# Second transformer layer: lane 1 of each turn four stages behind lane 0

## The chip, the core and the metric

The kernel runs on one core of one Trainium2 chip. The metric is the time of one execution on the device in microseconds; the median of the runs is taken. The engines of the core run their own instruction lists in order and meet only through semaphores: TensorE (PE), VectorE (DVE), ScalarE (ACT), GpSimd (POOL) and SyncE (SP), which issues most DMAs.

## What is computed

Two layers over an input x of 8 batches, 512 tokens and 256 features, in float32. The change touches the second layer alone, up to its end:

```python
# per batch: hidden 256, H = 16 heads of DH = 16, M = 64 random features
dg, db, ug, ub = cond @ (down_gamma, down_beta, up_gamma, up_beta)
h  = x + relu(x @ (down * dg + db)) @ (up * ug + ub)
q, k = feature_map(h @ Wq.T + bq), feature_map(h @ Wk.T + bk)   # exp(proj - norm) + 1e-6
v  = h @ Wv.T + bv
kv, ksum = k^T v, sum(k)             # per head
x  = x + (q @ kv / (q @ ksum)) @ Wo.T + bo
y  = x @ weight(cond) + bias(cond)
s  = max|y| / 127 per token;  y8 = round(y / s)
x  = x + (y8 @ Wq8) * s * weight_scale + bias
```

The first layer ends in a mixture of experts. Its last step, to add each token's two expert rows with their weights, is done by the second layer: it gathers the rows by index.

## The kernel before

After the first layer, `layer1` loads its weights and works through the 8 batches in four turns of two. A turn is `body(b2, more)`: three turns are a hardware loop with `more` true, the fourth stands behind it with `more` false. The two batches of a turn are lanes 0 and 1. Each lane has its own buffers and its own four PSUM banks; the lanes share no data, only the engines. A barrier of all engines ends each turn.

Each engine's part of a turn is a generator `lane(n, v, s)` that yields a stage number before it emits the instructions of that stage. `in_stages` (line 1560) makes one generator per lane and walks the stages: for each stage it lets lane 0 and then lane 1 emit what is due. So every engine's list is stage by stage, lane 0 ahead of lane 1 within a stage.

The stages, with their numbers: 0 transposes of x (line 1720), 1 down projection (1725), 2 up projection (1730), 3 and 4 the projections for K and Q (1742; ScalarE's biases and squares of Q in pieces of 32 partitions, line 1847), 5 V and the norms of K (1749, 1752), 6 to 9 the feature maps, two of eight parts a stage (TensorE 1766 and 1771, VectorE 1910, ScalarE's exponentials 1853 and 1855, the 1e-6 added by POOL at 1688 or VectorE at 1916 and 1919), 10 KV sums (1783), 11 their transposes (1790), 12 denominators and outputs (1797, 1802; VectorE's reciprocal 1941), 13 broadcast of the reciprocals (1808) and the product (1946), 14 output projection (1715), 15 transposes (1708), 16 the conditioned projection (1715) and VectorE's quantising block (1958 to 1970), 17 transposes of the quantised rows (1708), 18 the last projection (1715) and VectorE's scaling and sum (1974, 1978). `STAGES` is 19.

In a turn with `more`, the rows for the same lane's next batch are fetched: SP waits for the KV sums of lane 0, loads its indices and residual, then the same for lane 1 (lines 1666 to 1669). In stage 12 VectorE casts the indices (1581) and POOL issues eight indirect DMAs a lane (1588); in stage 16 VectorE adds the weighted rows ahead of the quantising block (1608); in stage 18 POOL waits for the transfers and resets them. SP stores lane 0's result, then lane 1's (1670 to 1674).

Of the kernel before, what the change touches and what calls it, by code (L numbers as in the profile page):

```python
# [55 lines left out]
def spread(ap, at, n, step=0):  # L56

    dims = [list(d) for d in ap.ap]
    dims.insert(at, [step, n])
    return bass.AP(ap.tensor, ap.offset, dims)  # L60
# [1445 lines left out]
ST_IN, ST_DN, ST_UP, ST_QK = range(4)  # L1506
ST_V, ST_KF = ST_QK + 2, ST_QK + 3
POOL_KF = (0, 2, 3, 5, 7)
QK_OUT = (2, 3, 0, 1, 2, 3)
ST_KV, ST_KVT, ST_O, ST_OT, ST_X3, ST_X3T, ST_Y, ST_Q, ST_ACC, STAGES = range(ST_KF + 4, ST_KF + 14)  # L1510

def layer1(nc, a, out, bank, ident, sb_in, Sems, chain_of, x1_d, gate_d, y_d, prow_d, wdec_d, PR, R1, n1):
# [3 lines left out]
    with l1:  # L1517
# [19 lines left out]
        LANES = 2  # L1537
# [22 lines left out]
        def in_stages(s, program):  # L1560

            live = [program(n, lane_bufs[n], lambda name, n=n: s(f"{name}_{n}")) for n in range(LANES)]
            due = [next(g) for g in live]
            for stage in range(STAGES):
                for n, g in enumerate(live):
                    while due[n] is not None and due[n] <= stage:
                        due[n] = next(g, None)  # L1570
            assert due == [None] * LANES

# [76 lines left out]
        def body(b2, more):  # L1649

            sctx = ExitStack()
            with sctx:
                s = Sems(sctx, "c")

                with nc.Block() as block:
# [20 lines left out]
                    @block.gpsimd  # L1676
                    def _(pool):
                        def lane(n, v, s):
                            yield ST_UP
                            pool.memset(v["kv"][:], 0.0).then_inc(s("kv0"), 1)  # L1680
                            pool.memset(v["kd"][:], 0.0).then_inc(s("kv0"), 1)
                            pool.tensor_tensor(v["xb"][:], v["x2"], spread(row("bo"), 1, T), ALU.add).then_inc(s("xb_ok"), 1)

                            for i in POOL_KF:
                                yield ST_KF + i // 2
                                pool.wait_ge(s("kf_in"), i + 1)
                                part = v["kf"][:, i // 2, 8 * (i % 2):8 * (i % 2) + 8, :]
                                pool.tensor_scalar(part, part, 1e-6, None, ALU.add).then_inc(s("kf_ok"), 1)  # L1688
                            yield ST_O
                            if more:  # L1690
                                gather_rows(pool, v, s)
                            yield ST_X3
                            pool.wait_ge(s("x3_ok"), 1)
                            pool.tensor_tensor(v["xb"][:], v["x3"], spread(row("bias"), 1, T), ALU.add).then_inc(s("x3b_ok"), 1)
                            yield ST_ACC
                            if more:
                                gathered(pool, s)
                        in_stages(s, lane)

                    @block.tensor  # L1700
                    def _(pe):
                        def lane(n, v, s):
# [31 lines left out]
                            for i in range(2 + 2 * K2):  # L1734
# [5 lines left out]
                                for m in range(K2):  # L1740
                                    w = wkv[:, 0, m, i * P:(i + 1) * P] if i < 2 else wqs[:, m, (i - 2) * P:(i - 1) * P]
                                    mm = pe.matmul(bk[QK_OUT[i]][:], w, v["hcT"][:, m, :], start=(m == 0), stop=(m == K2 - 1))  # L1742
                                mm.then_inc(s("qk_mm"), 1)
# [29 lines left out]
                            yield ST_KV  # L1773
                            pe.wait_ge(s("kf_ok"), len(POOL_KF))
                            pe.wait_ge(s("kf_ok2"), 8 - len(POOL_KF))
                            for g in range(2):
# [47 lines left out]
                            pe.wait_ge(s("qbT_ok"), 2)  # L1824
                            tokens_major(v["qbT"], wqb, "acc_mm")
                        in_stages(s, lane)

                    @block.scalar
                    def _(act):
                        def lane(n, v, s):  # L1830
# [9 lines left out]
                            for i in range(2 + 2 * K2):  # L1840
                                if i == 4:
                                    yield ST_QK + 1
                                if i >= 2:
                                    src = bk[QK_OUT[i]]
                                    act.wait_ge(s("qk_mm"), i + 1)
# [19 lines left out]
                            for m in range(K2):  # L1865
                                act.wait_ge(s("qbT_mm"), m + 1)
                                act.copy(v["qbT"][:, m, :], bk[m][:].bitcast(BF16)[:, 0:S]).then_inc(s("qbT_ok"), 1)
                        in_stages(s, lane)

                    @block.vector  # L1870
                    def _(dve):
                        def lane(n, v, s):
# [17 lines left out]
                            for i in range(2):  # L1890
                                dve.wait_ge(s("qk_mm"), i + 1)
                                dve.tensor_scalar(v["kT"][:, i, :], bk[QK_OUT[i]][:], kcol[:, i:i + 1], None, ALU.add).then_inc(s("ksq_ok"), 1)
                                dve.wait_ge(s("ksq_ok"), 2 * i + 1)
# [13 lines left out]
                            for i in range(8):  # L1907
# [4 lines left out]
                                                  spread(v["kn"][:, i // 2, i % 2, :], 2, M), ALU.add).then_inc(s("kf_sub"), 1)  # L1912
                                if i and i - 1 not in POOL_KF:
                                    dve.wait_ge(s("kf_in"), i)
# [190 lines left out]
```

## Time and profile before

| what | value |
|---|---|
| median of 3 runs | 3029.67 us (3029.49 to 3034.95) |
| the profiled execution | 3033.5 us, its span 3031.6 us |
| TensorE busy | 2256.5 us, 74% |
| VectorE busy | 1509.8 us, 50% |
| ScalarE busy | 1025.9 us, 34% |
| POOL busy | 890.6 us, 29% |
| mean granted clock of TensorE | 0.793 of full speed |
| turns of the second layer start at | 2456.3, 2604.0, 2750.8 and 2898.3 us |

Times in the rows are microseconds from the start of the span. A row of a timeline gives the start, the duration of the merged instructions, the engine, the line, what it writes and reads, how many instructions, and in brackets the idle time of that engine just before it with what ended it.
### The profile page before, as it was taken

Reading aid. Unit: us, or ns where it says so; the run is one execution under the profiler, and the core shown is the slowest. Engines: PE = TensorE matmul, PEld = TensorE weight load, DVE = VectorE, ACT = ScalarE, POOL = GpSimd, SP = SyncE. Lnnn points to the kernel's source line nnn. Section 1 sums busy time; section 2 is a strip of 40 time slices with the busy share of each in tenths; the row PEclk is TensorE's granted clock in tenths of the full one; section 3 lists DMA queues with packets and bytes.
Section 4 is the critical chain, followed back from the end, with each engine's and each line's share of the span. In section 5 each row is a group of like instructions: output and inputs, shape, how many; then the busy total and the mean of one; then the engine's idle time right before and its main releaser. Section 6 shows DMA issues by size and latency. Waiting matters only on the chain. (4 is left out here: it accounts for less than half of the span.)

```text
span 3031.6 us, 33534 instructions
## 1 busy us (share of the span) xinstructions
PE 2256.5 (74%) x11770; PEld 1421.0 (47%) x11770; DVE 1509.8 (50%) x3624; ACT 1025.9 (34%) x2535; POOL 890.6 (29%) x649
## 2 busy tenths in 40 slices
PE   6248877777777778768787777854999959686877
PEld 5125544444444444435444444432777725353544
DVE  2477576565655745746747556431111025453635
ACT  2015443333344334424334334431222233323332
POOL 0345252243334325324325223031000024040412
PEclk9577777778678678677677777876999979798989
DMA  6100010020010010010011002021322131010110
GB/s 216 37 16 1 21 58 1 15 72 7 15 59 20 15 58 22 8 65 22 1 56 37 1 15 70 1 65 37 112 94 94 59 97 43 29 42 29 42 30 15
DMA packets 62448, 128.67 MB, mean 42 GB/s; under 512 B 14420, under 2 KB 39114, under 8 KB 59858
## 3 DMA queue, kind: packets, MB, share of 16 engines
q1 hardware_dynamic: 46426, 76.32, 7.2%
q0 software_dynamic: 15872, 50.35, 5.6%
q8 instruction: 95, 1.56, 0.2%
q14 instruction: 55, 0.45, 0.1%
HBM read 97.17 MB, written 29.46 MB: 42 GB/s over the span
## 5 line engine op out<-in xcount | busy, mean ns | idle before, releaser
L1023 ACT ACTIVATE att_buf<-att_buf,nmin 128x384 f32<-128x384 f32 (+3 forms) x512 | 287.5, 562 | 771.4 <-DVE nmin L1338 764.1
L864 PE MATMUL bank<-kk,qT 32*128 32x512 f32 (+2 forms) x1024 | 356.7, 735 | 88.4 <-DVE nmin L1338 88.4
L695 POOL TENSOR_TENSOR big<-ex_at,kx 128x2048 f32<-128x2048 f32 x64 | 235.1, 3681 | 386.9 <-DVE xt_na L1132 313.1
L891 PE MATMUL bank<-ident,att_buf 128*128 128x128 f32 x1280 | 260.5, 343 | 56.8 <-ACT att_buf L1031 50.6
L1327 DVE TENSOR_TENSOR att_buf<-bank,wdiag 128x128 f32<-128x128 f32 x384 | 93.1, 284 | 322.0 <-PE bank L869 297.5
L644 POOL TENSOR_TENSOR big<-kx 128x1280 f32<-128x1280 f32 x64 | 162.6, 2567 | 300.3 <-ACT kx L963 291.2
L1132 DVE TENSOR_REDUCE xt_na<-big 128x64 f32<-128x1024 f32 x128 | 242.0, 1905 | 2.4 <-POOL big L695 1.6
L905 PE MATMUL bank<-att_buf,vp 128*32 128x128 f32 x2560 | 239.4, 329 | 0.0
L1031 ACT COPY att_buf<-bank 128x384 f32<-128x384 f32 (+3 forms) x512 | 208.6, 409 | 65.7 <-remote 40.7
L891 PEld LDWEIGHTS bank<-ident,att_buf 128*128 128x128 f32 x1280 | 190.2, 181 | 71.0 <-issue 42.5
L864 PEld LDWEIGHTS bank<-kk,qT 32*128 32x128 f32 x1024 | 118.5, 238 | 160.7 <-DVE nmin L1338 120.6
L905 PEld LDWEIGHTS bank<-att_buf,vp 128*32 128x32 f32 x2560 | 144.4, 128 | 65.9 <-issue 51.9
L1471 ACT ACTIVATE hid<-bank,eb 128x320 f32<-128x320 f32 x128 | 67.5, 527 | 241.6 <-PE bank L1446 241.6
L1446 PE MATMUL bank<-eb,ew 128*128 128x320 f32 x512 | 141.0, 437 | 1.7 <-DVE eb L1481 1.7
L1458 PE MATMUL bank<-ew,hid 128*128 128x256 f32 x640 | 139.6, 379 | 0.6 <-ACT hid L1471 0.6
L1338 DVE CUSTOM_DVE_ANT_0 att_buf<-bank,att_buf 128x128 f32<-128x128 f32 (+3 forms) x320 | 137.8, 446 | 0.0
L1688 POOL TENSOR_SCALAR kf<-kf 128x512 f32<-128x512 f32 x40 | 67.4, 1684 | 232.9 <-ACT kf L1853 231.9
L1458 PEld LDWEIGHTS bank<-ew,hid 128*128 128x128 f32 x640 | 121.0, 190 | 17.2 <-ACT hid L1471 1.1
L763 PE MATMUL bank<-cat,wint 128*128 128x512 f32 x256 | 119.2, 616 | 0.7 <-ACT cat L988 0.7
L1446 PEld LDWEIGHTS bank<-eb,ew 128*128 128x128 f32 x512 | 98.3, 192 | 42.4 <-DVE eb L1481 2.1
L856 PE MATMUL bank<-kk,qT 32*128 32x128 f32 x256 | 73.8, 379 | 57.9 <-DVE nmin L1338 31.2
L1111 DVE TENSOR_REDUCE big<-big 128x80 f32<-128x1280 f32 x64 | 86.4, 1349 | 47.2 <-POOL big L644 47.0
(339 smaller groups left out, 4049.2 us busy)
## 6 DMA issues: line engine op xcount, KB each, us to landing
ew<-in_eW SPq DMA_DIRECT2D x16, 1024.0 KB
buf_d<-zero SPq DMA_DIRECT2D x8, 640.0 KB, 7.9
er<-buf_d SPq DMA_DIRECT2D x8, 640.0 KB
y_d<-yy SPq DMA_DIRECT2D x8, 640.0 KB, 9.3
xt_na<-in_xT SPq DMA_DIRECT2D x8, 512.0 KB, 3.9
nA<-in_xN SPq DMA_DIRECT2D x8, 512.0 KB, 4.6
x_d<-x SPq DMA_DIRECT2D x8, 512.0 KB, 3.8
kf<-x_d SPq DMA_DIRECT2D x8, 512.0 KB, 3.2
```

Of the source, the lines that this page charges most:

```text
L644: pool.tensor_tensor(prod[:, lo:hi], spread(kx[:, t, 0:D], 1, hi - lo), spread(kx[:, t, DH * lo:DH * lo + D], 1, hi - lo, DH), ALU.mult)\
L695: pool.tensor_tensor(pv[:, :, c * P:(c + 1) * P].rearrange("p o (h d) -> p o h d", d=DH), spread(ex[:, t, :, 8 * c:8 * c + 8], 3, DH), spr ...
L763: mm = pe.matmul(bank[SIDE[o]][:], wint[:, order[n], o * P:(o + 1) * P], cat[:, n, :], start=(n == 0), stop=(n == 7))
L864: pe.matmul(bank[u % 2][:, 0:n], qT[r:r + 32, g, i * P:(i + 1) * P], kk[r:r + 32, g, T * i * P:T * i * P + n], start=True, stop=False)
L891: mm = pe.transpose(bank[3 + u % 2][:, j * P:(j + 1) * P], pr[:, u % NPR, j * P:(j + 1) * P], ident[:])
L905: mm = pe.matmul(bank[5][r:r + 32, i * P:(i + 1) * P], vp[:, j, p, DH * c:DH * c + 2 * DH], prT[:, (u + x) % 3, j * P:(j + 1) * P], start= ...
L1023: act.activation(pr[:, u % NPR, 0:n], pr[:, u % NPR, 0:n], ACT.Exp, scale=-1.0, bias=nmin[:, u % 4:u % 4 + 1], accum_out=rsum[:, i, h:h + ...
L1031: act.copy(prT[:, u % 3, 0:n], bank[3 + u % 2][:, 0:n]).then_inc(s("prT_ok"), 1)
L1132: dve.tensor_reduce(nA1[:, t, c * w:(c + 1) * w], pv[:, :, c * w:(c + 1) * w].rearrange("p o f -> p f o"), X, ALU.add).then_inc(s("pv_used ...
L1338: dve.tensor_tensor_reduce(dst if x else tiled(dst), lg[:, 0:n] if x else tiled(lg[:, 0:n]), add, 1.0, LARGE, ALU.add, ALU.min, nmin[:, (u ...
L1446: mm = pe.matmul(bank[n % 4][:, 0:W], ew1[:, k % 2, m, o * P:(o + 1) * P], eb[:, k % 2, m, c * W:(c + 1) * W], start=(m == 0), stop=(m == ...
L1458: mm = pe.matmul(bank[4 + n % 4][:, 0:D], hid[:, m, t * P:(t + 1) * P], ew2[:, k % 2, m, :], start=(m == 0), stop=(m == KH - 1))
```

## The change

`in_stages` shifts lane 1 by `LAG` = 4 stages: in its walk, lane n emits stage k when the walk is at k + 4n, and the walk is four stages longer. This holds for the lists of TensorE, ScalarE, VectorE and POOL. SP's list, the instructions themselves, their semaphores and buffers, and the order within each lane are as before.

```diff
 POOL_KF = (0, 2, 3, 5, 7)
+LAG = 4
...
-            for stage in range(STAGES):
+            for stage in range(STAGES + LAG * (LANES - 1)):
                 for n, g in enumerate(live):
-                    while due[n] is not None and due[n] <= stage:
+                    while due[n] is not None and due[n] + LAG * n <= stage:
                         due[n] = next(g, None)
```

## Rows read from the trace of the kernel before

**Rows 1.** The page's first part: TensorE's busy time and share of the span.
```profile
PE 2256.5 (74%) x11770; PEld 1421.0 (47%) x11770; DVE 1509.8 (50%) x3624; ACT 1025.9 (34%) x2535; POOL 890.6 (29%) x649
```

**Rows 2.** Windows, last turn: length, PE, PEld, DVE, ACT, POOL busy, clock, DMA, GB/s.
```profile
2898.30:3031.60 133.30, 111.31 (x656) 65.26 (x656) 62.71 (x114) 49.81 (x82) 27.21 (x18) 0.92 0.06 17
```

**Rows 3.** Timeline of TensorE in the third turn, loads of weights left out.
```profile
2751.07 3.67 PE L1708 MATMUL bank<-ident,kf 128*128 128x128 f32 x16 [9.37 <-PEq L100]
2757.80 5.88 PE L1725 MATMUL bank<-xT,wdn 128*64 128x512 f32 x8 [3.06 <-DVE wup L1883]
...
2767.25 3.70 PE L1742 MATMUL bank<-hcT,wkv 128*128 128x512 f32 x8
...
2774.22 3.60 PE L1742 MATMUL bank<-hcT,wkv 128*128 128x512 f32 x8
...
2790.80 0.67 PE L1749 MATMUL bank<-wkv,hcT 128*128 128x256 f32 x2 [2.68 <-ACT qs L1847]
...
2796.35 0.67 PE L1749 MATMUL bank<-wkv,hcT 128*128 128x256 f32 x2 [0.18 <-ACT qs L1847]
...
2801.58 1.10 PE L1766 MATMUL bank<-orfk,kT 128*128 128x512 f32 x2
...
2829.22 1.08 PE L1783 MATMUL bank<-kf,vn 128*32 128x128 f32 x32
...
2838.12 1.92 PE L1797 MATMUL bank<-qf,kd 128*32 128x512 f32 x16 [0.24 <-DVE kd L1934]
...
2855.20 10.20 PE L1715 MATMUL bank<-wo,xT 128*128 128x256 f32 x32 [4.48 <-DVE xT L1946]
...
2884.78 1.03 PE L1708 MATMUL bank<-identb,yb 128*128 128x128 bf16 x8 [7.32 <-DVE yb L1970]
```

**Rows 4.** Timelines of ScalarE and VectorE in that turn, and one group of VectorE's.
```profile
2779.57 16.63 ACT L1847 ACTIVATE qs<-bank,qscol 32x512 f32<-32x512 f32 x24 [1.34 <-PE bank L1742]
...
2840.12 3.36 DVE L1941 RECIPROCAL k<-bank 128x512 f32<-128x512 f32 x1 [0.84 <-PE bank L1797]
...
2879.86 1.28 DVE L1958 TENSOR_TENSOR qf<-bank,brow 128x512 f32<-128x512 f32 x2
...
2884.03 0.69 DVE L1970 TENSOR_SCALAR yb<-qf 128x1024 bf16<-128x1024 f32 x1
...
2892.08 1.23 DVE L1978 TENSOR_TENSOR qf<-qf,xb 128x1024 f32<-128x1024 f32 x1
...
L1919 DVE TENSOR_SCALAR qf<-qf 128x512 f32<-128x512 f32 x14 | 6.3, 448 | 0.1
```

**Rows 5.** Timelines of TensorE and VectorE in the last turn.
```profile
2898.45 3.67 PE L1708 MATMUL bank<-ident,kf 128*128 128x128 f32 x16 [9.44 <-PEq L100]
...
2985.01 1.92 PE L1797 MATMUL bank<-qf,kd 128*32 128x512 f32 x16 [0.24 <-DVE kd L1934]
...
2995.67 7.07 PE L1715 MATMUL bank<-wo,xT 128*128 128x256 f32 x32
...
3025.71 1.23 DVE L1978 TENSOR_TENSOR qf<-qf,xb 128x1024 f32<-128x1024 f32 x1
```

**Rows 6.** Waits: total us, times, longest; and POOL's first and last gather.
```profile
DVE xT L1946 <- remote: 27.2, 9, 5.2
ACT xT L1859 <- remote: 24.2, 6, 5.7
...
2839.55 1.04 POOL L1588 DMA_INDIRECT kf<-y_d,gidx  x1 [8.04 <-DVE gidx L1581]
...
2858.41 0.94 POOL L1588 DMA_INDIRECT kf<-y_d,gidx  x1 [0.30 <-issue]
```

**Rows 7.** Windows, as in rows 2, over most of the output projection.
```profile
2855.00:2862.00 7.00, 6.80 (x18) 5.42 (x18) 1.52 (x3) 0.00 (x0) 3.44 (x4) 0.55 0.38 96
```

**Rows 8.** Timelines of POOL and TensorE in layer 0, a run of eight transfers.
```profile
1971.01 1.03 POOL L704 DMA_INDIRECT buf_d<-nB,sidx  x1 [86.70 <-DVE sidx L1254]
...
1980.01 0.97 POOL L704 DMA_INDIRECT buf_d<-nB,sidx  x1 [0.30 <-issue]
...
1982.65 0.76 PE L856 MATMUL bank<-kk,qT 32*128 32x128 f32 x2 [4.84 <-remote]
```

## The prediction

> **What bounds the kernel now.** I read the page first, then the second layer alone, since the edit touches nothing else. TensorE is busy 74% of the span [rows 1], but that mixes two layers. The windows by turn narrow it: in the last of the four turns of the second layer TensorE is busy 111.3 of 133.3 us, VectorE 62.7, ScalarE 49.8 [rows 2]. So TensorE bounds the turns, and a lag of one lane can only win back what TensorE waits. The timeline of TensorE in a middle turn (the third) shows where that is [rows 3]. The turn runs from its first transpose at 2751.07 to the end of VectorE's last addition at 2892.08 + 1.23 = 2893.31 [rows 3, 4], which is 142.2 us. The last turn runs from 2898.45 to 3025.71 + 1.23 = 3026.94 [rows 5], 128.5 us, with the same matmuls. Between turns lie some 5 us that the edit leaves alone.
>
> Why is a loop turn 13.7 us longer than the last one? Only loop turns gather the rows for the next turn. From the first denominator matmul to the first matmul of the output projection a loop turn takes 2855.20 − 2838.12 = 17.1 us [rows 3], the last one 2995.67 − 2985.01 = 10.7 [rows 5]. In that stretch VectorE and ScalarE stand still with "remote" as releaser, 27.2 and 24.2 us in the three loop turns [rows 6], and there POOL issues its 16 gathers, 2839.55 to 2859.4 [rows 6]. Nothing else is new there, and the last turn, without gathers, has no such wait. I read it so: TensorE's signals to the other engines come late while gathers are under way. Then the projection itself takes 10.2 us where the last turn takes 7.1 [rows 3, 5], because the granted clock is 0.55 [rows 7], that is mostly the level of 1.2 GHz, after an idle stretch of 4.5 us. That is 6.4 + 3.1 us. The other 4.2 us are mainly the weighted sums of the gathered rows on VectorE, which stand ahead of the quantising block: TensorE waits 7.3 us for its second block [rows 3].
>
> **The change, part by part.** No instruction is added or removed. Lane 1's stage k now stands behind lane 0's stage k+4 in every engine's list. So in a turn lane 0 runs stages 0 to 3 alone, lane 1 its last four (output projection to accumulation) alone, and in between unlike stages meet.
>
> *TensorE's own work* stays. Per lane it is, from two-lane stretches halved: the first four projections 7.0 (2767.25 to 2774.22), V 5.5 (2790.80 to 2796.35), the feature maps 13.8 (2801.58 to 2829.22, two lanes) [rows 3]; all stages together some 54, so 108 for both.
>
> *The waits of TensorE, without gathers.* I laid the lists of the engines side by side with these durations, us from the turn's first transpose; a hand-off costs some 0.1 to 0.2. Lane 0's transposes end at 1.8. VectorE's weights are ready only at 6.7, as before (2757.80) [rows 3], so TensorE waits 4.9 where it waited 3.1: lane 1's transposes no longer fill it. Down and up projections now each expose their eviction, 0.9 and 0.9. The Q/K projections start at 13.8 and TensorE is through with them, and with lane 1's transposes, at 25.2. ScalarE needs 16 pieces of 16.63/24 = 0.69 us [rows 4], 11.1 in all, from 19.2 on, so V of lane 0 waits until 30.3: 5.2 us (it was 2.7 [rows 3]). Then the lanes overlap. ScalarE has lane 1's 11.1 us of pieces with lane 0's exponentials between them, and V of lane 1 waits 1.8. Feature maps, KV sums and outputs keep TensorE fed until 109.6. Now VectorE's order decides: lane 0's quantising block takes 4.9 (2879.86 to 2884.03 + 0.69), and lane 1's reciprocal of 3.36 stands behind it [rows 4]. TensorE waits 1.7 and 2.4. From 118.1 lane 1 is alone: projection 3.5, VectorE 1.3 exposed, transposes 1.1, copy 0.6, the next projection 3.5, the whole quantising block 4.9, transposes, copy 0.7, accumulation, and VectorE's last 2.9. End at 138.8. The waits are 4.9 + 0.9 + 0.9 + 5.2 + 1.8 + 1.7 + 2.4 + 1.3 + 0.6 + 4.9 + 0.7 + 2.9 = 28.2, against 128.5 − 111.3 = 17.2 now. 11.0 more, less 0.9 since lane 1's transposes meet the full clock: the last turn gets slower by some 10.3.
>
> *SP.* It waits for lane 1's KV sums only after lane 0's, and for lane 0's end before lane 1's; all its transfers have 15 us or more of slack. No cost; without this slack the 3.2 us landing of a 512 KB row load would show.
>
> *POOL.* Lane 0's eight gathers move from beside lane 1's to the feature maps of lane 1, with two of lane 1's additions (1.7 each) behind them. These are due only at lane 1's KV sums, some 12 us later. Nothing, or 2 if the gathers come late.
>
> *The weighted sums* of lane 0 now lie beside its own next projection and lane 1's outputs, those of lane 1 beside a projection: hidden, gain up to 4.2 per loop turn. What is late next is the quantising block itself, counted above.
>
> *The gathers.* This is the disputed term. Two groups of eight, about 30 us apart, take the place of one of sixteen. The nearest rows are in layer 0, where eight indirect transfers in a row (1971.01 to 1981.0) are followed by a TensorE wait of 4.84 us on "remote", ended at 1982.65 [rows 8]. Lower bound per group: 0, as matmuls of the other lane may hide it. Upper: 6.3, the time from the end of what was released to the end of the outage for lane 1's projection, and 3.5 of half clock behind it. I take 4.8 for each group, since rows 8 is the same run of eight beside busy matmuls, and one slow-clock stretch of 3.1 for both, as now [rows 3, 5]. A loop turn then takes 138.8 + 9.6 + 3.1 = 151.5, 9.3 more than now.
>
> Beside this, VectorE's additions of 0.45 us [rows 4] would now run during lane 0's gathers; the gathers' pitch beside busy VectorE in layer 0 is 1.27 us [rows 8], as against 1.25 in rows 6, so I add nothing. The Trainium skill (SBUF — State Buffer, Who interferes with whom) says that a VectorE copy, cast or tensor_scalar in a two-port mode holds the port pair that GpSimd needs, also to write descriptors. An estimate by it: six additions in the way, 2.7 us per loop turn, would give 3076. The rows above don't bear it out.
>
> **The sum.** 3 × 9.3 + 10.3 = 38.2. The profiled execution took 3033.5 us (span 3031.6); with the change it would take 3071.7. The median of the runs is 3.8 lower, 3029.67, which gives 3068.
>
> **The rivals.** *1: the gathers are covered.* With only eight of them and the other lane's matmuls between, the outage costs nothing. A loop turn is 138.8, 3.4 less than now; 3 × −3.4 + 10.3 = 0.1: 3030, no change. For it: the lane that isn't gathering has work. Against: in that work each matmul pair waits for the evictions two pairs earlier, so late signals stop it too, and rows 8 shows just that. 0.10.
>
> *2: the outage spreads.* The feature maps signal every 0.86 us, the stretch that is hit today much less often. If each group stops TensorE for 10 us, plus a slow clock behind each (3.1), a loop turn takes 138.8 + 20 + 6.2 = 165, 22.8 more: 3 × 22.8 + 10.3 = 78.7, 3108. Against: in rows 8 the outage ends with the run of transfers. 0.10.
>
> *3: faster.* The one mechanism is full cover: in the overlapped stretch there is always a matmul of the other lane in front of TensorE, so that its waits there (1.8 + 1.7 + 2.4 = 5.9) and the outages vanish. A loop turn is 132.9, 9.3 less, the last turn 4.4 more: −23.5, 3006. It decides in favour when the gain per loop turn passes 5.5 us, (10.3 + 6)/3. Against: an engine takes its list in order, and the list puts lane 0's next stage, not any ready matmul, in front. 0.05. The Trainium skill (Perfetto Trace Analysis, Optimization Strategy) says that where the most-contended engine changes over time, interleaving the regimes may help; this is that rule, and this kernel's stages do change from ScalarE to TensorE to VectorE. But TensorE is already busy 87% of the last turn.
>
> *4: the edit does little.* The lag exposes only the head and tail and the gathers cost what they cost today: 138.8 + 6.4 + 3.1 = 148.3, 6.1 more, 3 × 6.1 + 10.3 = 28.6: 3058. 0.20.
>
> **Chances and range.** My forecast has 0.55. A measurement of this kernel tells about 0.2%, 6 us, from no change. Slower by more than that: the forecast, rivals 2 and 4, 0.85, and a rest of 0.01 of rival 1; same: 0.08; faster: 0.06, rival 3 and a little of rival 1. The range goes from 3038 (loop turns as now, only the last turn's 10.3 with a little less) to 3094: outages at their upper bound in every group, 138.8 + 2 × (6.3 + 3.5) = 158.4, 16.2 more, gives 3 × 16.2 + 10.3 = 58.9, 3089, and 5 for exposed hand-offs.
>
> **What would show it.** Turns: last turn 138.8, loop turns 151.5 from first transpose to last addition. V of lane 0 should start 30.3 after the first transpose with a wait of about 5 on ScalarE. The "remote" waits should appear twice a loop turn, once amid feature maps, once at the reciprocal's broadcast of lane 1. One VectorE block of 4.9 should stand with TensorE idle near the end of every turn. The prediction is wrong if the last turn isn't slower (then my hand schedule of head and tail fails), or if loop turns beat 142 us (then the gathers are covered).

## The result and the profile after

The changed kernel takes 3082.66 us (median of 4 runs, 3079.36 to 3087.42) where the kernel before takes 3032.31: a ratio of 1.0125, 95% interval 1.0087 to 1.0163. It is slower. By the medians the loss is 50 us, by the profiled executions 54; the ratio on record puts it lower, at 38 us (26 to 49), and the medians' own quotient, 1.0166, lies just outside its interval. So the size of the loss is known to some 15 us, its sign is certain. The forecast was 3068, range 3038 to 3094. The time lies in the range and the sign is right, but two terms of the sum were wrong and cancelled in the loop turns, as the turns show.

All of the difference lies in the four turns of the second layer. From first transpose to last addition they took 142.5, 141.6, 142.2 and 128.5 us before, and 152.7, 151.9, 152.0 and 151.8 after: 53.6 us more, of 53.8 by which the span grew (3085.4 against 3031.6). The forecast had 151.5 for a loop turn and 138.8 for the last.

The last turn as windows: length, PE, PEld, DVE, ACT and POOL busy with instruction counts, granted clock, DMA share, GB/s. The first row is the last turn of the kernel before, from first transpose to last addition ([rows 2] runs 5 us further, to the end of the span). The second is the whole turn of the changed kernel; the others are its head, the stretch to V of lane 0, V of lane 0 with lane 1's down projection, the overlapped part, and the end.

```profile
2898.45:3026.94 128.49, 111.31 (x656) 65.25 (x656) 62.71 (x114) 49.81 (x82) 27.07 (x18) 0.94 0.05 14
...
2929.00:3080.90 151.90, 123.69 (x656) 70.04 (x656) 62.90 (x114) 49.56 (x82) 26.11 (x18) 0.85 0.04 12
...
2929.00:2944.70 15.70, 9.38 (x16) 3.47 (x16) 2.62 (x6) 1.77 (x3) 2.69 (x3) 0.50 0.24 76
2944.70:2962.90 18.20, 12.91 (x32) 6.08 (x33) 4.03 (x8) 11.00 (x17) 0.00 (x0) 0.88 0.01 1
2962.90:2974.30 11.40, 11.40 (x36) 8.70 (x36) 1.42 (x3) 0.95 (x2) 0.00 (x0) 0.62 0.00 0
2974.30:3048.50 74.20, 71.15 (x497) 39.12 (x496) 38.48 (x73) 32.62 (x55) 21.06 (x14) 1.00 0.00 1
3048.50:3080.90 32.40, 18.85 (x76) 12.67 (x76) 16.35 (x25) 3.22 (x6) 2.36 (x1) 0.74 0.05 16
```

The same 656 matmul instructions are busy for 123.7 us where they were for 111.3, at a mean clock of 0.85 instead of 0.94. The whole head runs at 0.50, the level of 1.2 GHz; V of lane 0 has 0.62. And TensorE waits 151.9 − 123.7 = 28.2 us (28.1 if the window ends with the last addition), the sum of waits that the prediction worked out; before it was 17.2. TensorE's timeline shows the waits one by one, and they answer to [rows 3, 5]:

```profile
2929.01 1.96 PE L1709 MATMUL bank<-ident,kf 128*128 128x128 f32 x8 [8.11 <-PEq L100]
2935.84 3.65 PE L1726 MATMUL bank<-xT,wdn 128*64 128x512 f32 x4 [4.87 <-DVE wup L1884]
2940.17 3.78 PE L1731 MATMUL bank<-dT,wup 64*128 64x512 f32 x4 [0.68 <-ACT dT L1839]
2944.73 5.17 PE L1743 MATMUL bank<-hcT,wkv 128*128 128x512 f32 x8 [0.78 <-DVE hcT L1889]
2962.90 1.19 PE L1750 MATMUL bank<-wkv,hcT 128*128 128x256 f32 x2 [5.26 <-ACT qs L1848]
3002.13 0.67 PE L1750 MATMUL bank<-wkv,hcT 128*128 128x256 f32 x2 [1.40 <-ACT qs L1848]
...
3048.51 0.62 PE L1709 MATMUL bank<-identb,yb 128*128 128x128 bf16 x8 [1.39 <-DVE yb L1971]
3051.78 3.78 PE L1809 MATMUL bank<-k,sel 128*128 128x512 f32 x4 [2.64 <-DVE k L1942]
3062.01 1.09 PE L1709 MATMUL bank<-ident,qf 128*128 128x128 f32 x8 [1.38 <-DVE qf L1952]
3063.83 5.37 PE L1716 MATMUL bank<-wde,hcT 128*128 128x256 f32 x16 [0.73 <-ACT hcT L1864]
3074.16 1.04 PE L1709 MATMUL bank<-identb,yb 128*128 128x128 bf16 x8 [4.96 <-DVE yb L1971]
```

The brackets, with one of 0.74 before the last projection and 2.9 us of VectorE at the end that aren't shown, read 4.87, 0.68, 0.78, 5.26, 1.40, 1.39, 2.64, 1.38, 0.73 and 4.96; for these the forecast had 4.9, 0.9, 0.9, 5.2, 1.8, 1.7, 2.4, 1.3, 0.6 and 4.9. What it didn't have are the durations. The up projection takes 3.78 us for four instructions, where eight took 3.7 at the full clock; V shows 1.19 for two instructions where [rows 3] has 0.67; lane 1's conditioned projection takes 5.37 for sixteen, where thirty-two of the same shape, in the output projection, took 7.07 at the full clock [rows 5].

The gathers, which should have cost a loop turn 12.7 us, cost nothing: loop turns and last turn are equally long. In the list of waits, the two rows of [rows 6] are gone, while layer 0 in the same execution still has its waits on "remote" (total, times, longest):

```profile
ACT att_buf L1031 <- remote: 40.1, 11, 6.0
DVE att_buf L1327 <- remote: 21.6, 7, 3.6
PE bank L856 <- remote: 4.9, 1, 4.9
```

### The profile page after: what moved, and what is told of

It reads as the page before. It is cut to its first block and busy times, and to the rows that moved or that the text cites. A ratio compares the mean times of both kernels' runs of the same rounds, so it can differ in the third digit from the quotient of the medians.

```text
span 3085.4 us, 33534 instructions
## 1 busy us (share of the span) xinstructions
PE 2289.9 (74%) x11770; PEld 1430.4 (46%) x11770; DVE 1513.4 (49%) x3624; ACT 1025.3 (33%) x2535; POOL 891.1 (29%) x649
## 5 line engine op out<-in xcount | busy, mean ns | idle before, releaser
L1458 PE MATMUL bank<-ew,hid 128*128 128x256 f32 x640 | 139.6, 379 | 0.6 <-ACT hid L1471 0.6
L1458 PEld LDWEIGHTS bank<-ew,hid 128*128 128x128 f32 x640 | 121.0, 190 | 17.2 <-ACT hid L1471 1.1
```

Source lines behind the costliest of these rows:

```text
L1458: mm = pe.matmul(bank[4 + n % 4][:, 0:D], hid[:, m, t * P:(t + 1) * P], ew2[:, k % 2, m, :], start=(m == 0), stop=(m == KH - 1))
```

## The experiments

Two questions follow. Is it the slow clock that makes each turn 13 us longer than the hand schedule, or the hand-offs? And when do the late signals of TensorE beside gathers occur? The twelve runs were made on three chips, four kernels on each: e1 to e4 on chip A, e5 to e8 on chip B, e9 to e12 on chip C. Each ratio is against the kernel before on the same chip. A kernel with no ratio was timed once. The last turn has no gathers; in the kernel before it took 128.5 us in the first comparison, 128.4 on chip B and 128.5 on chip C, so it can be compared across chips.

**Filling the waits** (e1_fill). Matmuls into a bank that nobody reads stand where TensorE would wait.

```diff
+def filler(count, dst):
+    for _ in range(count):
+        pe.matmul(dst[:], wkv[:, 0, 0, 0:P], wqs[:, 0, :], start=True, stop=True)
...
 yield ST_DN
+if n == 0:
+    filler(3, bank[7])
...
 yield ST_V
+if n == 0:
+    filler(6, bank[7])
...
 yield ST_OT
+if n == 1:
+    filler(3, bk[3])
...
 yield ST_Q
+if n == 1:
+    filler(5, bank[0])
```

> The changed kernel with filler matmuls whose result nobody reads: 3 before lane 0's down projection, 6 before lane 0's V, 3 before lane 1's broadcast of reciprocals, 5 before lane 1's last transposes; each stands where TensorE waits anyway. Theory (half clock): in the changed kernel every turn takes 152 us where the hand schedule at full clock has 138.8, because the waits drop the granted clock and V of lane 0 takes 9.6 us instead of 5.3, the first projections 3.6 more, the last stages some 5 more. With the waits filled V of lane 0 should take about 5.3 again, a turn 141 to 145 us, the whole 3085 - 4 x 9 = about 3048. Rival (the waits and hand-offs themselves, not the clock, cost the 13 us): the turn stays at 151 to 153 or grows by the fillers, the whole 3083 or more.

Measured: 2983.9 us against 2988.7, ratio 0.9986 (0.9963 to 1.0008): nearly the whole loss is gone. The changed kernel without fillers wasn't run on this chip; on the others its turns took 150 to 153 us. The turns take 138.2, 137.6, 137.7 and 137.1 us, less than expected. Windows of its last turn, cut at the same places as above:

```profile
2832.80:2844.60 11.80, 9.46 (x23) 4.24 (x23) 2.62 (x6) 1.76 (x3) 2.55 (x2) 0.84 0.33 102
2844.60:2861.30 16.70, 16.60 (x45) 7.62 (x46) 4.03 (x8) 11.10 (x17) 0.00 (x0) 1.00 0.00 0
2861.30:2868.50 7.20, 7.20 (x37) 5.38 (x38) 1.42 (x3) 0.88 (x3) 0.00 (x0) 1.00 0.00 0
2868.50:2940.00 71.50, 69.83 (x488) 38.85 (x492) 36.08 (x65) 31.40 (x53) 21.06 (x14) 1.00 0.00 1
2940.00:2970.00 30.00, 21.65 (x104) 12.88 (x96) 18.73 (x33) 4.39 (x8) 2.35 (x1) 1.00 0.05 18
```

The head falls from 15.7 to 11.8 us though three fillers (six instructions) stand in it, with the clock at 0.84; V falls from 11.4 to 7.2, at 1.00. TensorE does more work and is done sooner. So the hand schedule's 138.8 was close for a full clock (137.1 measured; its head was 1.8 us too long, with V at 30.3 where it starts at 28.5 here), and the missing 13 us are the half clock. The Trainium skill (TensorE: Matmul & The Clock Gate, What's actually happening) says that the throttled state is the default and activity releases it; these two sets of windows agree, 0.50 in the head without and 0.84 with fillers.

**Which filler does it** (e9_fill_v): the six before lane 0's V alone.

> The changed kernel with fillers at one place only, 6 matmuls before lane 0's V, where TensorE waits 5.3 us for ScalarE. Theory (the wait drops the clock for what follows): from the start of V to the first feature map it takes some 7 us instead of 11.5 to 13; the start of V itself (33.9) and the stretch at the end of the turn are as in the changed kernel. A turn takes 152 - 5 = 147 us. Rival (the fillers of the head did it, V's clock follows from the head): V to feature maps stays at 11 us or more, a turn 151.

Measured: 3025.19 us against a median of 2990.7. The windows of V in the last turn and of the whole turn:

```profile
2907.60:2914.80 7.20, 7.17 (x37) 5.37 (x37) 1.42 (x3) 0.98 (x2) 0.00 (x0) 1.00 0.00 0
2873.70:3018.50 144.80, 122.32 (x668) 67.20 (x668) 62.89 (x114) 49.48 (x82) 26.09 (x18) 0.90 0.04 13
```

V has its 7.2 us at 1.00, and V starts at 33.9, as without fillers: the slow clock follows the wait that stands right before it. The rival falls. The loop turns take 148.2 to 148.7, the last 144.8, around the expected 147. One part of the expectation failed: the end of the last turn, which the edit doesn't touch, took 29.5 us at a clock of 0.84 instead of 32.4 at 0.74; lane 1's conditioned projection had the full clock there, 3.72 us instead of 5.37, behind the same waits. So these later waits don't drop the clock to the same extent in each turn.

**Fillers without the lag** (e7_before_fill): the kernel before with 2, 3, and 2 and 5 fillers at its own waits (before the down projection, before V, before each lane's last transposes). Those before V stand behind a wait for ScalarE's first squares of Q.

> The kernel before (no lag) with filler matmuls whose result nobody reads at TensorE's waits: 2 before lane 0's down projection, 3 before lane 0's V, 2 and 5 before the transposes of the quantised rows of lanes 0 and 1. Theory (the slow clock costs wherever a wait stands): the head's down projection, which runs at half clock, gets 2 to 3 us shorter, the last transposes and projection 1 to 2: 3 to 5 us a turn, the whole 12 to 20 us less, ratio 0.993 to 0.996. Against the changed kernel with fillers (ratio 0.9986) it then shows what the lag itself costs at a full clock: some 10 to 20 us. Rival (fillers help only where a lane is alone): ratio 0.999 to 1.003.

Measured: 3027.27 us against 3044.84, ratio 0.9953 (0.9924 to 0.9981). The last turn takes 126.1 us at a clock of 0.99, 2.4 less than without fillers, a little under the expected 3 to 5; the loop turns, with late signals, take 139.6 to 141.0. This is the second half of the answer: with the clock held, the lag costs 137.1 − 126.1 = 11.0 us in the last turn (two chips, and not the same number of fillers); the forecast said 10.3.

**Smaller doses** (e2_lag2, e12_lag1): `LAG = 2` and `LAG = 1`.

> The changed kernel with a lag of 2 stages instead of 4. Theory: what costs is the stretch that a lane runs alone and the slow clock behind its waits. With 2 stages lane 1's output projection to conditioned projection has lane 0's stages beside it, only transposes and last projection stay alone, so about 5 us of the 10 of the tail come back; the wait for lane 0's Q pieces stays. Last turn about 143 to 147 us (before 128.5, lag 4: 151.8). Gathers: lane 1's output matmuls, which write 32 partitions each, now fall into lane 0's run of eight; if late signals come from such matmuls beside gathers, loop turns are some 5 us longer than the last turn and late signals are seen again; if they depend on the number of transfers in a row, they stay away. The whole 3060 to 3085.

Measured: ratio 1.0074 (1.0046 to 1.0101); last turn 139.8 us, better than expected, loop turns 147.1, 143.4 and 146.4. No wait on "remote" anywhere in its trace, nor in the other three of chip A, in layer 0 either: that chip doesn't show the late signals, so the part of the question on gathers stayed without an answer.

> The changed kernel with a lag of 1 stage. Lane 0 runs only its transposes alone, lane 1 only its last projection. Theory: the last turn costs some 3 to 6 us more than without lag (128.5), from the wait for lane 0's Q pieces (TensorE has less of lane 1 to do) and from the last projection alone; loop turns depend on the chip as for lag 0, but lane 1's output matmuls again lie near lane 0's gathers. Ratio 0.998 to 1.008. The doses 1, 2 and 4 should rise in this order if the stretch that a lane runs alone is what costs.

Measured: ratio 0.9972 (0.9952 to 0.9993), just below the expected range; last turn 133.7, loop turns 138.1 to 139.1. The last turns rise with the dose, 128.5, 133.7, 139.8, 151.8 for lags 0, 1, 2 and 4, as expected. That the lag of 1 is not slower in the medians isn't explained by its one profile: its turns add up to 549.7 us, those of the kernel before on the same chip to 546.0.

**Gathers elsewhere** (e3_before_late, e4_lag4_late). POOL's gathers move three stages down, the weighted sums behind the lane's last addition.

```diff
-yield ST_O
-if more:
-    gather_rows(pool, v, s)
 yield ST_X3
 pool.wait_ge(s("x3_ok"), 1)
 pool.tensor_tensor(v["xb"][:], v["x3"], spread(row("bias"), 1, T), ALU.add).then_inc(s("x3b_ok"), 1)
+yield ST_X3T
+if more:
+    gather_rows(pool, v, s)
...
 yield ST_Y
-if more:
-    combine(dve, v, s)
...
 dve.tensor_tensor(fo, fo, v["xb"][:], ALU.add).then_inc(s("fin"), 1)
+if more:
+    combine(dve, v, s)
```

With the lag, lane 0's weighted sums stand one stage further down still, so that they don't hold up lane 1.

> The kernel before (no lag) with both lanes' gathers issued three stages later, behind POOL's last addition (stage 15), and the weighted sums of the gathered rows moved behind the last addition of the turn. Same 16 transfers in a row. Theory A (the late signals of TensorE need the output matmuls beside the gathers): the stretch from denominators to output projection falls from 17.1 to 10.7 us and the projection from 10.2 to 7.1; the weighted sums move to the end and cost up to 6.5 us there, part of it behind the store: loop turn 135 to 141 us, the whole 3005 to 3030. Theory B (16 transfers in a row delay TensorE's signals wherever they stand): the same loss of 6 us and more appears at the quantising block's transposes and the last projection; loop turn 142 or more, the whole 3030 to 3050.

Measured: 2979.22 us, ratio 0.9962 (0.9935 to 0.9989); loop turns 133.1, 144.8 and 133.2. The 144.8 is a slow clock behind V's wait of 2.69 us: the stretch from V to the feature maps takes 20.5 us in that turn, 10.8 to 12.1 in the others. The 17.1 us stretch is 10.7 and the projection 7.07, as theory A wants, but on a chip where no signal is late at all, so this doesn't tell A from B.

> The changed kernel (lag 4) with the gathers of each lane issued three stages later (stage 15) and the weighted sums behind the lane's last addition. Lane 0's run of eight now lies beside lane 1's output matmuls (TensorE's stage 12 of lane 1), lane 1's run beside its own last stages. Theory A (gathers beside output matmuls): TensorE's signals of lane 1's denominators and outputs come 2 to 6 us late, with waits on remote, loop turn some 3 to 6 us longer than in the changed kernel. Theory B (16 in a row are needed): no late signal, loop turn as in the changed kernel, 152, or 2 longer for lane 1's weighted sums at the end.

Measured: 3033.49 us, turns of 150.6, 150.7, 151.6 and 151.6, no late signal. Inconclusive for the same reason.

**The kernel before and after, unchanged, on other chips** (e5_before, e6_after, e10_before, e11_after).

> The kernel before, unchanged, looked at beside the others on their chip. The four kernels of the first call showed no late signal of TensorE beside any gather, not in layer 0 either, and ran some 45 us faster than the first comparison would have it. Theory C (late signals belong to the chip or its state, not to the kernel): if this chip is like that one, a loop turn takes 17.1 - 10.7 + 3.1 = 9 us less than the 142 of the first trace, and the whole about 2990. Theory D (they belong to this order of instructions): loop turns of 142 us and waits on remote in the stretch from denominators to output projection, on this chip too.

> The changed kernel, unchanged, on the same chip. In the first trace it showed no late signal in the second layer; its turns all took 152 us. Theory C: on a chip without late signals its turns stay near 150 to 152, while those of the kernel before fall to about 133, so that the loss grows from 50 us to some 3 x 18 + 23 = 70 to 77: ratio 1.022 to 1.026. Theory D: the loss is again about 50 us, ratio 1.013 to 1.018.

Measured on chip B: before 3031.08, turns 142.9, 142.4, 141.0 and 128.4, with waits on "remote" as in the first comparison:

```profile
ACT att_buf L1031 <- remote: 40.5, 12, 5.9
DVE xT L1946 <- remote: 29.2, 10, 5.2
ACT xT L1859 <- remote: 26.2, 6, 5.7
```

After 3081.51, ratio 1.0121 (1.0085 to 1.0156), turns 150.0, 151.7, 151.9 and 151.7, and again no such wait in the second layer.

> The kernel before, unchanged, for its profile on this chip. Theory C, as it stands now (late signals of TensorE belong to the chip: seen on the first chip and on that of the second call, in no kernel of the first call): either late signals in layer 0 and in the second layer's loop turns (142 us) together, or in neither, and then loop turns of 131 to 134 us. A mixed picture, late signals in layer 0 but not in the second layer of this kernel, would speak against it.

> The changed kernel, unchanged, on the same chip as the kernel before. On a chip with late signals ratio 1.010 to 1.016, as twice before. On a chip without them its turns stay at 150 to 152 while the kernel before gets faster: ratio 1.018 to 1.026.

Measured on chip C: before 2980.93, turns 136.8, 135.8, 144.9 and 128.5, and no wait on "remote" in the whole trace. Its gathers stand where they always stood, and TensorE goes straight on, to be held against [rows 3, 6]:

```profile
2792.13 1.92 PE L1797 MATMUL bank<-qf,kd 128*32 128x512 f32 x16 [0.23 <-DVE kd L1934]
2802.79 7.07 PE L1715 MATMUL bank<-wo,xT 128*128 128x256 f32 x32
...
2793.56 1.04 POOL L1588 DMA_INDIRECT kf<-y_d,gidx  x1 [8.03 <-DVE gidx L1581]
2812.37 1.21 POOL L1588 DMA_INDIRECT kf<-y_d,gidx  x1 [0.30 <-issue]
```

10.7 us instead of 17.1, with the same 16 gathers under way. The loop turns are longer than the 131 to 134 expected of a chip without late signals. After: 3041.63, ratio 1.016 (1.0118 to 1.0202), turns 151.0 to 151.4. So theory C holds as far as it goes: in the kernel before, late signals come in layer 0 and the second layer together, or in neither, by chip. That the loss is larger without them is not shown: the ratio is higher than 1.0121 and 1.0125, but the intervals overlap, and it is below the 1.018 expected. One thing that makes the kernel before slower here is the third turn of its profile, where V's wait of 2.68 us dropped its clock too; how often that happens in the other executions isn't known. The window over V, 18.9 us against 10.8 to 12.1 in its other turns:

```profile
2735.30:2754.20 18.90, 18.90 (x65) 16.35 (x65) 1.63 (x4) 5.10 (x8) 0.00 (x0) 0.54 0.00 0
```

**No lag, late gathers and fillers** (e8_before_late_fill).

> No lag, the gathers three stages later with the weighted sums at the end of the turn (as in the third experiment, ratio 0.9962), and the fillers. If both gains are apart they add: ratio 0.989 to 0.992, a loop turn 129 to 131 us. If the fillers only replace what the late gathers gave (both shorten the same wait at the quantising block), the ratio is that of the fillers alone or 0.2% below it.

Measured on chip B, which has late signals: 3023.09 us, ratio 0.9922 (0.9886 to 0.9959), loop turns 139.2 to 139.8 instead of the expected 129 to 131, last 125.9. The stretch from denominators to projection is clean now, but the late signals came back at the new place. A wait of ScalarE of 13.61 us, which the profile puts down to a transfer of layer 0 that had long ended, and TensorE's wait behind it:

```profile
2876.40 1.07 ACT L1877 COPY qbT<-bank 128x512 bf16<-128x512 bf16 x2 [13.61 <-DMA gac<-in_ms,ids]
...
2877.53 1.89 PE L1719 MATMUL bank<-wqb,qbT 128*128 128x256 bf16 x8 [10.21 <-ACT qbT L1877]
```

The transposes for which ScalarE waits were issued at 2865.8. So moving the gathers pays on a chip without late signals (e3) and only shifts the loss on one with them; of the 0.78% here, the fillers alone had given 0.47%, and the two intervals overlap. It has the lowest ratio of all kernels that were run, and its interval lies below 1.

## Why the prediction was right, and where it wasn't

**TensorE's waits without gathers: right.** 28.2 us forecast, 28.2 measured in the last turn, and no single one off by more than 0.4. The lag costs 11.0 us in the last turn at a full clock, 10.3 were forecast. The prediction's terms don't quite add up among themselves: 11.0 less 0.9 is 10.1 and not 10.3, and "some 54, so 108 for both" isn't what its 138.8 contains, which without the waits is 110.6 us of work.

**The clock: missed.** The step that failed is "TensorE's own work stays". It charged one stretch of 3.1 us at half clock, behind the gathers, and none for the new waits. Measured are 123.7 us of work instead of 110.6, some 13 us in each turn, loop or not (151.8 in the last against the hand schedule's 138.8). In the last turn: 3.6 us up to V (33.9 instead of 30.3), 4.2 in V and the down projection behind it (45.3 − 33.9 = 11.4, where it is 7.2 with fillers), some 2 at the broadcast of the reciprocals (3.78 us instead of 1.9) and 3 from lane 1's output projection to the end. The sign was there to be read: [rows 3] has the head's eight down-projection instructions at 5.9 us, where eight of the up projection, as long, took 3.70 at the full clock (2763.62), and [rows 7] has the half clock behind a wait of 4.5 us; the schedule made waits of 4.9, 5.2 and 4.9 us and left their wake out.

**The gathers: wrong.** The step "I take 4.8 for each group" took a run of eight in layer 0 for the price of a run of eight in the second layer. Measured: nothing, in both comparisons in which the kernel before shows late signals. Rival 1 was right on this term. Its reason (matmuls of the other lane hide it) isn't what the trace shows: the signals aren't late there. Nor do they follow the number of transfers: layer 0's runs of eight still have them (and the 4.84 us of [rows 8] lie from 1977.81 on, most of them beside the transfers and not behind them), and in the kernel before ScalarE's late copy at 2848.20, after 5.30 us on "remote", stands ahead of the ninth gather at 2849.66.

**The weighted sums: right.** They are hidden; loop turns are no longer than the last.

**POOL: right.** Lane 1's last two additions came behind lane 0's gathers, at 2874.11, and lane 1's KV sums still started without a wait at 2877.31. The turns leave no room for a cost on SP either. The estimate by the Trainium skill (SBUF — State Buffer, Who interferes with whom), 2.7 us a loop turn, isn't borne out: eight gathers beside VectorE's additions took 10.0 us, 2864.08 to 2873.10 + 0.94, one of them 1.09 instead of 0.95, where lane 1's eight, from 2892.09 to 2900.95 + 0.94, took 9.8. (The pitch in layer 0 that the prediction held against it is 1.29 us by [rows 8] and not 1.27.)

**The sum.** Forecast 3 × 9.3 + 10.3 = 38.2; measured by the traces 10.2 + 10.3 + 9.8 + 23.3 = 53.6. The loop turns are right to about 1 us by two errors that cancel (−12.7 for gathers, +13 for the clock), the last turn, which has no gathers to cancel with, is off by its whole 13. The time lay in the range by luck: because the upper bound of the gathers had been taken in, not because the clock had been thought of.

**Open.** Why TensorE's signals are late beside indirect transfers in the first comparison and on chip B (which may be the same chip), and on chips A and C never; and why, where they are late, some places are hit (denominators and outputs without lag, the last transposes in e8) and others never (the lagged kernel's feature maps), was not settled. A loop turn without gathers on a chip with late signals wasn't tried.

## What to carry to other kernels

When two streams that share an engine are set apart, write down the new waits of the bounding engine one by one, and then charge each long one twice: once for itself, and once for the slow clock of the work behind it, which here came to as much again (11.0 us of added waits and 13 of slow clock a turn). A stream that saturates the bounding engine together with its twin (87% here) has little to win from a lag and pays head and tail in every turn that ends with a barrier. A few matmuls into a free bank at the longest waits cost nothing here: they gave 0.5% without the lag, and with it the ratio was 0.9986, where the lag alone had 1.012 to 1.016 on other chips.

## What the runs showed of the hardware

TensorE's clock fell behind the 5.3 us wait before V in each of the 12 turns of the changed kernel in its three profiles (V and the down projection took 8.8 to 13.3 us where they take 7.2 with fillers), and behind the kernel before's wait of 2.68 us in some turns and not in others (18.9 us in e10_before's third turn, 10.8 in its second); with fillers in the waits its mean over the last turn was 0.99 (126.1 us of e7_before_fill, 137.2 us of e1_fill).

On chip B other engines that wait for TensorE started up to some 10 us after its matmuls had ended in the trace (2865.8 + 0.6 to 2876.4 in e8_before_late_fill), in stretches in which POOL issues indirect transfers. That it is the semaphore signal which is late is read from this, not measured by itself. Both profiles of the first comparison and all four of chip B show such waits, none of the eight of chips A and C, the unchanged kernel being run on B and C. The medians of the kernel before are 3032 and 3045 us where it is seen and 2989 and 2991 where it isn't, 41 to 56 us apart. Little of this lies in the second layer: the spans of e5_before and e10_before are 3029.1 and 2978.9 us, and their second layer's first transposes start at 2453.9 and 2412.5, so 41 of the 50 us stand ahead of it. Whether other differences of the chips have a share wasn't separated.
